# First layer: the next tile's rows turned behind the first gate half, loaded ahead of the weights, their row weights picked at the clip; the head norm behind the outputs

## The chip, the core and the metric

The kernel runs on one core of a Trainium2 chip. Times are device microseconds (us) of one execution. The engines are PE (matmul, with its weight loads shown as PEld), DVE (vector), ACT (scalar), POOL (GpSimd) and SP, which issues most of the DMAs. Every engine works through its own list of instructions in order; a semaphore wait holds back everything behind it on that engine. The clock of PE has two levels here, 2.4 GHz (shown as 1.00) and 1.2 GHz (0.50).

## What is computed

Two transformer layers over 4096 tokens (8 batches of 512) of width 256. Cut to what matters here:

```python
xn = layernorm(x)
x = x + L0_attn(xn) + L0_ffn(xn)     # first layer
xn = layernorm(x)
x = x + L1_attn(xn) + L1_ffn(xn)     # second layer

def L0_ffn(x):                       # 8 experts, 4 per token
    gate, up = split(x @ gate_up_proj[e] + bias[e])
    gate = minimum(gate, 7.0); up = clip(up, -7.0, 7.0)
    act = (up + 1.0) * gate * sigmoid(1.702 * gate)
    return sum over the chosen e of combine[n, e] * (act @ down_proj[e] + down_bias[e])
```

L0_attn is a causal softmax attention of 16 heads of 16 dimensions, whose queries and keys are normalized per head (the head norm of the title).

## The kernel before

**Steps.** The attention of the whole program is cut into 192 steps: step G is batch n = G // 8 and pair of heads p = G % 8 (the first 64 steps are the first layer's attention). The tokens of the first layer's experts lie sorted by expert in 71 tiles of 256 rows. The tiles are worked on inside the steps 21 to 49: `pipeline` writes a list `plan` of 15 pieces for each step, in six parts. The pieces of tile s are, in this order: gate half 0, up half 0, gate half 1, down half 0 of tile s-1, up half 1, down half 1 of tile s-1. As 15 pieces are two and a half tiles, the steps alternate: an **even** step (22, 24, ... 48) has the parts [down 1, gate 0], [up 0, gate 1, down 0], [up 1, down 1], [gate 0, up 0, gate 1], [down 0, up 1], [down 1, gate 0, up 0]; an **odd** one (23, 25, ... 49) [gate 1, down 0], [up 1, down 1, gate 0], [up 0, gate 1], [down 0, up 1, down 1], [gate 0, up 0], [gate 1, down 0, up 1]. Even steps have p = 6, 0, 2, 4, odd ones p = 7, 1, 3, 5.

**PE** (`pair_with_experts` in its part of `pipeline`) does in a step: `shifted` (turns the queries, source qst), `outputs_by_rows` (turns the last step's outputs, source oT), part 0, three score units (L605), `turn_qk` (turns the next step's queries, qst, and keys, kst), part 1, the other scores, part 2 and so on, then `outputs` (L681), the last part, and in the middle of that, for p = 1 to 4, `project` (L628, two matmuls for the next batch). With p = 1 it also turns the next batch's rows (`turn_rows`, source xb) behind the outputs. A gate or up half is `up()`: 12 matmuls (L539) into the bank of gate or up; a down half is 12 matmuls (L559).

**Two banks for everything that is turned.** All turns and projections write to the ring X, which in these steps has only the two PSUM banks 0 and 1, taken by turns (`take`). PE waits at each until the engine that reads the bank has let go of what was there before.

**The next tile's rows.** `turn_x(s+1)` turns the rows of the next tile (source xs, L513) into such a bank behind up half 0 of tile s. ACT copies them (`take_x`, xh), and DVE then subtracts (`rest`, xl, L1648), which frees the bank.

**DVE** does for a tile half g: `clip_gate` (L1660), `clip_up` (L1674) and `multiply` (L1683, L1686), where `multiply` runs in `finish()`, ahead of the next gate half's clip or at fixed places of the step. Behind the multiply of half 0 `finish` does `rest(s+1)`, behind that of half 1 `pick_weight(s+1)` (L1640, L1643), which waits for the gate and up weights of tile s+1 (tile gu). In a step: `heads_out` (L1931 to L1937, frees the bank of the turned outputs), for p = 0 `context_out` (L1945) and `row_stats` (L1729 on), the parts 0 and 1, ..., maxima of the scores (L1845), `shift`, the rest of the parts, and at the end for p = 0 `normalize` (L1747, four instructions on xb) and for p = 5 and 6 `norm_heads` (L1794, L1799, L1802; 4 heads, then 12).

**SP** issues the loads: rows of tile s+2 (xs) at up half 0, its gate and up weights (gu, 2 MB, once the multiply of half 1 of tile s is done) at up half 1, its down weights (dn) and the store of the outputs (ys) at down half 1.

Of the kernel before, what the change touches and what calls it, by code (L numbers as in the profile page):

```python
# [34 lines left out]
H, HD = 16, 16  # L35
# [113 lines left out]
def build(nc, dram, outs, ctx):  # L149
# [232 lines left out]
    def pipeline(kinds, its, mems, em=None, general=False):  # L382
# [39 lines left out]
        def last_tile(s):  # L422
            return s + 1 in (FIRST_TILE[1], FIRST_TILE[1] + TILES[1])

        def tiles_to(s):
            return FIRST_TILE[layer_of(s)] + TILES[layer_of(s)]
# [65 lines left out]
        with block as block:  # L492

            @block.tensor
            def _(pe):
# [25 lines left out]
                def up(s, m, side):  # L521
# [18 lines left out]
                                           x[s % 2][:, TS * k:TS * (k + 1)],  # L540
                                           start=(n == 0), stop=(n == len(terms) - 1))
                    mm.then_inc(full, 1)
                    if m == 0 and side == 1 and not last_tile(s):
                        turn_x(s + 1)

                def down(s, half):
# [351 lines left out]
            def _(sp):  # L898
# [55 lines left out]

                def experts(G, q, some=slice(None)):
                    for what, s, i in plan[G][q][some]:
                        if what == "up" and s + 2 < tiles_to(s):
                            if i == 0:
                                load_x(s + 2)
                            else:  # L960
                                load_up(s + 2)
                        if what == "down" and i == 1:
                            if s + 2 < tiles_to(s):
                                load_down(s + 2)
                            store_y(s)
# [399 lines left out]
            def _(act):  # L1365
# [38 lines left out]

                def experts(G, q, some=slice(None)):
                    for what, s, i in plan[G][q][some]:
                        if what == "up":
                            highs()
                            gate(2 * s + i)
                            late.append(2 * s + i)  # L1410
                            if i == 0 and not last_tile(s):
                                take_x(s + 1)
                        elif what == "down":
                            highs()
                            take_y(s, i)
# [214 lines left out]
            def _(dve):  # L1630
# [65 lines left out]
                def experts(G, q, some=slice(None)):  # L1696
                    for what, s, i in plan[G][q][some]:
                        if what == "gate":
                            finish()
                            if layer_of(s) == 0:  # L1700
                                clip_gate(2 * s + i)
                        if what == "up":
                            if layer_of(s) == 0:
                                clip_up(2 * s + i)
                            late.append((s, i))

                def finish():

                    while late:
                        s, i = late.pop(0)  # L1710
                        multiply(2 * s + i)
                        if not last_tile(s):
                            if i == 0:
                                rest(s + 1)
                            else:
                                pick_weight(s + 1)
# [397 lines left out]
                def pair_with_experts(G):  # L2114
# [2 lines left out]
                        heads_out(G - 1)  # L2117
                    if is_at(n - 1, "mla") and p == 0:
                        context_out(n - 1)
                    if G in begins:  # L2120
                        rest(FIRST_TILE[begins.index(G)])
                        pick_weight(FIRST_TILE[begins.index(G)])
# [20 lines left out]
                        residual(n - 1)  # L2143
                    if n + 1 < nb and p == 0:
                        normalize(n + 1)
                    if is_at(n + 1, "mla"):
                        if p == 5:
                            norm_heads(n + 1, slice(0, 4))
                        if p == 6:
                            norm_heads(n + 1, slice(4, H))  # L2150

                def pair_alone(G):
                    n, p = divmod(G, NP)
# [321 lines left out]
```

## Time and profile before

| | us |
|---|---|
| median of 3 runs | 3187.16 |
| lowest and highest | 3186.24, 3191.06 |
| profiled execution, whole | 3193.81 |
| profiled execution, span of the core | 3192.2 |
| PE busy in the span | 2821.9 (88%) |
| DVE busy | 2168.8 (68%) |
| ACT busy | 1621.9 (51%) |
| POOL busy | 1496.9 (47%) |

Times of the trace are counted from the start of the span. The first layer's expert steps, 21 to 49, lie between 430 and about 1350 us. A line of the timeline is a group of like instructions in a row: its start, the time from its start to its end, engine, line, operation, output<-input, shapes and count, and in brackets how long the engine stood idle before it and what ended that.

### The profile page before, as it was taken

Reading aid. Unit: us, or ns where it says so; the run is one execution under the profiler, and the core shown is the slowest. Engines: PE = TensorE matmul, PEld = TensorE weight load, DVE = VectorE, ACT = ScalarE, POOL = GpSimd, SP = SyncE. Lnnn points to the kernel's source line nnn. Section 1 sums busy time; section 2 is a strip of 40 time slices with the busy share of each in tenths; the row PEclk is TensorE's granted clock in tenths of the full one; section 3 lists DMA queues with packets and bytes.
Section 4 is the critical chain, followed back from the end, with each engine's and each line's share of the span. In section 5 each row is a group of like instructions: output and inputs, shape, how many; then the busy total and the mean of one; then the engine's idle time right before and its main releaser. Section 6 shows DMA issues by size and latency. Waiting matters only on the chain. (4 is left out here: it accounts for less than half of the span.)

```text
span 3192.2 us, 60490 instructions
## 1 busy us (share of the span) xinstructions
PE 2821.9 (88%) x20990; PEld 2283.0 (72%) x20990; DVE 2168.8 (68%) x6229; ACT 1621.9 (51%) x3388; POOL 1496.9 (47%) x2213
## 2 busy tenths in 40 slices
PE   3878789999999999978898889898799999999986
PEld 2555478888989898846666666666588888888864
DVE  4777678778778787756777777766645554454576
ACT  1544444544444454445655555555455555555553
POOL 3586753353343353375556666322233333333487
PEclk8877799999999999989999999999899999999998
DMA  2564567778777787522333444210365555565445
GB/s 81 179 218 165 199 246 290 276 280 320 281 283 285 280 298 297 216 40 51 94 93 106 107 107 107 91 67 21 134 221 207 212 214 211 199 234 204 134 96 123
DMA packets 192066, 580.08 MB, mean 182 GB/s; under 512 B 22856, under 2 KB 144656, under 8 KB 157456
## 3 DMA queue, kind: packets, MB, share of 16 engines
q1 hardware_dynamic: 154896, 525.03, 44.6%
q0 software_dynamic: 36864, 51.14, 7.8%
q8 instruction: 172, 2.82, 0.3%
q14 instruction: 134, 1.10, 0.1%
HBM read 450.14 MB, written 125.96 MB: 180 GB/s over the span
## 5 line engine op out<-in xcount | busy, mean ns | idle before, releaser
L1157 POOL TENSOR_TENSOR al<-t,ah 128x512 fp32r<-128x512 f32 x220 | 285.5, 1298 | 865.9 <-ACT ah L1389 865.9
L539 PE MATMUL bank<-xh,gu 128*128 128x256 f32 x3520 | 658.0, 291 | 22.7 <-DMA gu<-wu_scratch 7.0
L584 PE MATMUL bank<-masks_bf,ident_bf 128*128 128x128 bf16 x1896 | 433.3, 252 | 131.8 <-DVE st L1845 41.4
L1845 DVE TENSOR_REDUCE st<-bank 128x1 f32<-128x512 f32 (+3 forms) x1024 | 422.7, 480 | 181.8 <-PE bank L602 152.9
L539 PEld LDWEIGHTS bank<-xh,gu 128*128 128x128 f32 x3520 | 512.8, 192 | 45.1 <-issue 19.1
L1486 ACT ACTIVATE pt<-bank 128x512 f32<-128x512 f32 (+1 forms) x1152 | 512.3, 541 | 47.5 <-PE bank L605 40.2
L1494 ACT ACTIVATE oT<-bank 128x512 f32<-128x512 f32 x192 | 114.5, 597 | 615.3 <-PE bank L681 581.9
L584 PEld LDWEIGHTS bank<-masks_bf,ident_bf 128*128 128x128 bf16 x1896 | 170.5, 99 | 356.5 <-DVE st L1845 99.7
L602 PE MATMUL bank<-ksT,qsT 128*128 128x512 f32 (+3 forms) x1536 | 412.6, 369 | 5.8 <-DVE top L1843 3.2
L605 PE MATMUL bank<-qaT,ksT 128*128 128x512 f32 (+3 forms) x1536 | 402.7, 372 | 0.0
L539 PE MATMUL bank<-xl,gu 128*128 128x256 f32 x1760 | 354.6, 283 | 0.0
L602 PEld LDWEIGHTS bank<-ksT,qsT 128*128 128x128 f32 x1536 | 279.2, 203 | 27.8 <-DVE top L1843 17.1
L513 PE MATMUL bank<-ident,qst 128*128 128x128 f32 x1536 | 239.3, 284 | 57.8 <-POOL kst L1209 35.4
L1389 ACT ACTIVATE ah<-t 128x512 fp32r<-128x512 f32 x220 | 138.7, 630 | 286.9 <-DVE t L1686 249.6
L539 PEld LDWEIGHTS bank<-xl,gu 128*128 128x128 f32 x1760 | 273.7, 192 | 0.0
L605 PEld LDWEIGHTS bank<-qaT,ksT 128*128 128x128 f32 x1536 | 267.9, 201 | 6.1
L1843 DVE MAX8 top<-bank 128x8 f32<-128x512 f32 (+3 forms) x512 | 213.7, 483 | 72.7 <-PE bank L602 50.1
L681 PE MATMUL bank<-pt,V 128*17 128x512 f32 (+3 forms) x3072 | 261.0, 460 | 0.7 <-ACT pt L1486 0.7
L559 PE MATMUL bank<-dn,ah 128*128 128x256 f32 x1760 | 257.0, 288 | 0.0
L513 PEld LDWEIGHTS bank<-ident,qst 128*128 128x128 f32 x1536 | 184.9, 146 | 91.5 <-issue 41.0
L559 PEld LDWEIGHTS bank<-dn,ah 128*128 128x128 f32 x1760 | 224.7, 191 | 4.6 <-issue 3.7
L1262 POOL DMA_INDIRECT acc<-ys_scratch,slots x128 | 203.5, 1590 | 45.0 <-issue 39.2
(254 smaller groups left out, 5247.0 us busy)
## 6 DMA issues: line engine op xcount, KB each, us to landing
gu<-wu_scratch SPq DMA_DIRECT2D x110, 2056.0 KB, 8.0
dn<-wd_scratch SPq DMA_DIRECT2D x110, 1024.0 KB, 9.7
xs<-xs_scratch SPq DMA_DIRECT2D x110, 264.0 KB, 9.0
ys_scratch<-yb SPq DMA_DIRECT2D x110, 256.0 KB, 9.9
raw<-in_gu SPq DMA_DIRECT2D x16, 1024.0 KB
wu_scratch<-hi SPq DMA_DIRECT2D x16, 1024.0 KB
wu_scratch<-lo SPq DMA_DIRECT2D x16, 1024.0 KB
xs_scratch<-empty SPq DMA_DIRECT2D x32, 264.0 KB
```

Of the source, the lines that this page charges most:

```text
L513: mm = pe.transpose(bank[:, P * n:P * (n + 1)], b, ident[:, :])
L539: mm = pe.matmul(bank[:, TS * h:TS * (h + 1)], gu[:, col:col + P], x[s % 2][:, TS * k:TS * (k + 1)], start=(n == 0), stop=(n == len(terms) ...
L559: mm = pe.matmul(down_bank[:, D * half:D * (half + 1)], a[s % 2][:, j // 2, tok:tok + P], dn[:, part + D * j:part + D * (j + 1)], start=(n ...
L584: return pe.matmul(S.bank((which, G, u))[:, diag:diag + P * len(unit)], ident_bf[:, :], masks_bf[:, side, 0:len(unit), :].rearrange("p n k ...
L602: mm = pe.matmul(bank[:, first:first + width], mem["qsT"][:, P * blk:P * (blk + 1)], ks[:, 0:width], start=begin, stop=end, skip_group_che ...
L605: mm = pe.matmul(bank[:, first:first + width], ks[:, P * blk:P * (blk + 1)], mem["qaT"][:, T - width:T], start=begin, stop=end, skip_group ...
L681: mm = pe.matmul(bank[q0:q0 + HD + 1, P * kb:T], V[n % 2][:, kb, vh, :], pt[:, j, PT_AT[kb]:PT_AT[kb] + T - P * kb], start=(kb < 2), stop= ...
L1157: pool.tensor_tensor(em["al"][s % 2][:, m, :], em["t"][g % 2][:, :], em["ah"][s % 2][:, m, :].bitcast(F32), ALU.subtract).then_inc(al_read ...
L1262: pool.indirect_dma_start(acc[:, NT * b + t, :], None, ys_dram, at, compute_op=ALU.add).then_inc(gathered[i], 16)
L1486: act.activation(to, frm, ACT.Relu if kind == "spm" else ACT.Exp).then_inc(s_act, 1)
L1843: ins = dve.max(top[:, 0, r, :], bank[:, first:first + width])
L1845: ins = dve.reduce_max(st[:, 0, r:r + 1], bank[:, first:first + width], AX.X)
```

## The change

- `turn_x(s+1)` stands behind gate half 0 of tile s instead of up half 0 (first layer only), and `take_x` on ACT moves with it, ahead of that half's tanh.
- On DVE `rest(s+1)` comes right behind `clip_gate` of half 0, and `pick_weight(s+1)` right behind `clip_up` of half 1, ahead of the multiply of that half; `finish` does neither in the first layer any more.
- SP loads the rows of tile s+3 at up half 1 of tile s, ahead of the weights of tile s+2.
- `norm_heads` of the next batch moves from the end of the steps p = 5 and 6 to the steps p = 6 and 7, behind `heads_out` (and `context_out`).

```diff
@@ PE, up() @@
-                    if m == 0 and side == 1 and not last_tile(s):
+                    if m == 0 and side == layer_of(s) and not last_tile(s):
                         turn_x(s + 1)
@@ SP, experts() @@
-                        if what == "up" and s + 2 < tiles_to(s):
-                            if i == 0:
-                                load_x(s + 2)
-                            else:
+                        if what == "up" and i == 0 and (layer_of(s) or s == 0) and s + 2 < tiles_to(s):
+                            load_x(s + 2)
+                        if what == "up" and i == 1:
+                            if layer_of(s) == 0 and s + 3 < tiles_to(s):
+                                load_x(s + 3)
+                            if s + 2 < tiles_to(s):
                                 load_up(s + 2)
@@ ACT, experts() @@
+                        if what == "gate" and i == 0 and layer_of(s) == 0 and not last_tile(s):
+                            highs()
+                            take_x(s + 1)
                         if what == "up":
                             highs()
                             gate(2 * s + i)
                             late.append(2 * s + i)
-                            if i == 0 and not last_tile(s):
+                            if i == 0 and layer_of(s) and not last_tile(s):
                                 take_x(s + 1)
@@ DVE, experts() and finish() @@
                                 clip_gate(2 * s + i)
+                                if i == 0 and not last_tile(s):
+                                    rest(s + 1)
                         if what == "up":
                             if layer_of(s) == 0:
                                 clip_up(2 * s + i)
+                                if i == 1 and not last_tile(s):
+                                    pick_weight(s + 1)
                             late.append((s, i))
...
-                        if not last_tile(s):
+                        if layer_of(s) and not last_tile(s):
                             if i == 0:
                                 rest(s + 1)
@@ DVE, pair_with_experts() @@
                     if is_at(n - 1, "mla") and p == 0:
                         context_out(n - 1)
+                    if is_at(n + 1, "mla"):
+                        if p == 6:
+                            norm_heads(n + 1, slice(0, 4))
+                        if p == 7:
+                            norm_heads(n + 1, slice(4, H))
...
-                    if is_at(n + 1, "mla"):
-                        if p == 5:
-                            norm_heads(n + 1, slice(0, 4))
-                        if p == 6:
-                            norm_heads(n + 1, slice(4, H))
```

**PE, start of an even step.** From the end of gate half 0 in part 0 (into bank2) over the first scores to up half 0 (bank3). Before:

```order
L539 MATMUL bank2<-xh1_103,gu1_107 128x256 x2
L605 MATMUL bank5<-qaT_57,ksT00_53 128x512
L605 MATMUL bank6<-qaT_57,ksT00_53 128x128
L605 MATMUL bank6<-qaT_57,ksT00_53 128x384
L605 MATMUL bank7<-qaT_57,ksT00_53 128x256
L513 MATMUL bank1<-ident,qst1_50 128x128 x4
L513 MATMUL bank0<-ident,kst_51 128x128 x4
L539 MATMUL bank3<-xh1_103,gu1_107 128x256 x2
```

Now:

```order
L539 MATMUL bank2<-xh1_103,gu1_107 128x256 x2
L513 MATMUL bank1<-ident,xs0_100 128x128 x4
L605 MATMUL bank5<-qaT_57,ksT00_53 128x512
L605 MATMUL bank6<-qaT_57,ksT00_53 128x128
L605 MATMUL bank6<-qaT_57,ksT00_53 128x384
L605 MATMUL bank7<-qaT_57,ksT00_53 128x256
L513 MATMUL bank0<-ident,qst1_50 128x128 x4
L513 MATMUL bank1<-ident,kst_51 128x128 x4
L539 MATMUL bank3<-xh1_103,gu1_107 128x256 x2
```

The turn of xs moved ahead of the scores. It takes bank1, the bank that the queries took, so that the queries now take bank0, which the outputs (oT) had, and the keys (kst) take bank1, which xs has.

**PE, end of an even step with a projection.** From the last matmuls of gate half 0 over L628 to the first turns of the next step. Before:

```order
L539 MATMUL bank2<-xh1_103,gu1_107 128x256 x2
L628 MATMUL bank0<-w_mla_72,xT 128x512
L628 MATMUL bank1<-w_mla_72,xT 128x512
L539 MATMUL bank3<-xh1_103,gu1_107 128x256 x2
L539 MATMUL bank3<-xl1_105,gu1_107 128x256 x2
L539 MATMUL bank3<-xh1_103,gu1_107 128x256 x4
L539 MATMUL bank3<-xl1_105,gu1_107 128x256 x2
L539 MATMUL bank3<-xh1_103,gu1_107 128x256 x2
L513 MATMUL bank0<-ident,xs0_100 128x128 x4
L513 MATMUL bank1<-ident,qst1_50 128x128 x4
L513 MATMUL bank0<-ident,oT_59 128x128 x4
```

Now:

```order
L539 MATMUL bank2<-xh1_103,gu1_107 128x256 x2
L513 MATMUL bank0<-ident,xs0_100 128x128 x4
L628 MATMUL bank1<-w_mla_72,xT 128x512
L628 MATMUL bank0<-w_mla_72,xT 128x512
L539 MATMUL bank3<-xh1_103,gu1_107 128x256 x2
L539 MATMUL bank3<-xl1_105,gu1_107 128x256 x2
L539 MATMUL bank3<-xh1_103,gu1_107 128x256 x4
L539 MATMUL bank3<-xl1_105,gu1_107 128x256 x2
L539 MATMUL bank3<-xh1_103,gu1_107 128x256 x2
L513 MATMUL bank1<-ident,qst1_50 128x128 x4
L513 MATMUL bank0<-ident,oT_59 128x128 x4
```

The second of the two projections (L628) now takes bank0, which xs took just ahead; the outputs (oT) at the start of the next step take a bank that the projection had, where before they took that of xs.

**DVE, from the last multiply of a step with p = 5 into the step with p = 6.** Before:

```order
L1683 SCALAR_TENSOR_TENSOR gc_92<-th_93,gc_92 128x512
L1686 SCALAR_TENSOR_TENSOR t1_95<-t1_95,gc_92 128x512
L1640 TENSOR_TENSOR wtmp_99<-xs1_101,gu1_107 128x16
L1643 TENSOR_REDUCE wsel2_98<-wtmp_99 128x2
L1794 TENSOR_TENSOR qk_mla0_66<-qk_mla0_66,qkn_73 128x4x64 x2
L1799 TENSOR_TENSOR qk_mla0_66<-qk_mla0_66,qkw_74 128x4x64 x2
L1802 TENSOR_TENSOR qk_mla0_66<-qk_mla0_66 128x4x64
L1931 COPY both_65<-bank0 128x136
L1932 TENSOR_TENSOR both_65<-both_65,bank0 128x102
L1936 RECIPROCAL rec_64<-both_65 128x8
L1937 TENSOR_TENSOR ctxt1_62<-both_65,rec_64 128x4x32
L1660 TENSOR_SCALAR gc_92<-bank2,gu1_107 128x256 x2
```

Now (the lines of the file have moved by 5 to 9):

```order
L1688 SCALAR_TENSOR_TENSOR gc_92<-th_93,gc_92 128x512
L1691 SCALAR_TENSOR_TENSOR t1_95<-t1_95,gc_92 128x512
L1940 COPY both_65<-bank0 128x136
L1941 TENSOR_TENSOR both_65<-both_65,bank0 128x102
L1945 RECIPROCAL rec_64<-both_65 128x8
L1946 TENSOR_TENSOR ctxt1_62<-both_65,rec_64 128x4x32
L1803 TENSOR_TENSOR qk_mla0_66<-qk_mla0_66,qkn_73 128x4x64 x2
L1808 TENSOR_TENSOR qk_mla0_66<-qk_mla0_66,qkw_74 128x4x64 x2
L1811 TENSOR_TENSOR qk_mla0_66<-qk_mla0_66 128x4x64
L1665 TENSOR_SCALAR gc_92<-bank2,gu1_107 128x256 x2
L1653 TENSOR_TENSOR xl0_104<-bank1,xh0_102 128x512
L1679 TENSOR_SCALAR t0_94<-bank3,gu1_107 128x256 x2
```

The two rows of `pick_weight` (wtmp, wsel) now stand just ahead of these rows, ahead of the multiply (gc, t) and behind the clip of the up half; `heads_out` (both, rec, ctxt) stands ahead of the head norm (qk_mla); and xl stands behind the clip of the gate half, with the head norm, the multiply and `heads_out` all in front of it.

## Rows read from the trace of the kernel before

**Rows 1.** who PE waited for between 430 and 1345 us: total, times, longest.

```profile
PE bank L513 <- DVE xl L1648: 28.8, 14, 2.1
PE bank L513 <- DVE both L1932: 9.6, 7, 1.6
PE bank L539 <- DMA gu<-wu_scratch: 7.0, 8, 1.8
PE bank L539 <- DVE gc L1660: 6.9, 16, 1.6
PE bank L513 <- DVE xb L1747: 3.9, 3, 2.7
```

**Rows 2.** windows: length, busy us (instructions) by engine, PE clock, DMA share, GB/s.

```profile
430.00:1345.00 915.00, 856.59 (x6960) 805.00 (x6961) 709.03 (x1621) 439.59 (x863) 361.76 (x473) 0.98 0.75 282
...
755.00:759.00 4.00, 4.00 (x35) 3.92 (x33) 3.96 (x4) 0.84 (x2) 1.52 (x1) 1.00 0.93 376
...
821.00:825.00 4.00, 4.00 (x23) 4.00 (x22) 0.85 (x3) 1.70 (x3) 1.27 (x1) 0.58 0.87 329
```

**Rows 3.** timeline, PE, step 21.

```profile
439.48 0.66 PE L513 MATMUL bank<-ident,kst 128*128 128x128 f32 x4 [1.38 <-DVE xl L1648]
```

**Rows 4.** timeline, DVE, from step 30 into step 31 (p = 7).

```profile
752.49 0.68 DVE L1683 SCALAR_TENSOR_TENSOR gc<-th,gc 128x512 f32<-128x512 f32 x1
...
753.82 0.68 DVE L1648 TENSOR_TENSOR xl<-bank,xh 128x512 fp32r<-128x512 f32 x1
...
754.42 2.91 DVE L1794 TENSOR_TENSOR qk_mla<-qk_mla,qkn 128x768 f32<-128x768 f32 x2
...
760.10 0.29 DVE L1931 COPY both<-bank 128x136 f32<-128x136 f32 x1
...
761.29 0.88 DVE L1660 TENSOR_SCALAR gc<-bank,gu 128x256 f32<-128x256 f32 x2
```

**Rows 5.** timeline, PE, step 49 (p = 1), with no xs turned before it.

```profile
1338.07 1.16 PE L513 MATMUL bank<-ident,xb 128*128 128x128 f32 x8 [2.71 <-DVE xb L1747]
```

**Rows 6.** timeline, PE and DVE, start of step 30 (p = 6).

```profile
723.85 0.50 PE L539 MATMUL bank<-xh,gu 128*128 128x256 f32 x2 [0.28 <-DMA gu<-wu_scratch]
...
723.90 0.17 DVE L1640 TENSOR_TENSOR wtmp<-xs,gu 128x16 f32<-128x16 f32 x1 [0.40 <-DMA gu<-wu_scratch]
...
724.20 1.85 DVE L1794 TENSOR_TENSOR qk_mla<-qk_mla,qkn 128x256 f32<-128x256 f32 x2
...
727.22 0.29 DVE L1931 COPY both<-bank 128x136 f32<-128x136 f32 x1
...
727.86 0.66 PE L513 MATMUL bank<-ident,kst 128*128 128x128 f32 x4 [1.25 <-DVE both L1932]
```

**Rows 7.** timeline, PE and DVE, start of step 32 (p = 0).

```profile
787.86 0.50 PE L539 MATMUL bank<-xh,gu 128*128 128x256 f32 x2 [0.76 <-DMA gu<-wu_scratch]
...
789.22 0.29 DVE L1931 COPY both<-bank 128x136 f32<-128x136 f32 x1
...
793.59 0.88 DVE L1660 TENSOR_SCALAR gc<-bank,gu 128x256 f32<-128x256 f32 x2
...
794.52 0.51 PE L539 MATMUL bank<-xh,gu 128*128 128x256 f32 x2 [1.59 <-DVE gc L1660]
```

**Rows 8.** timeline, POOL, DVE and PE, start and end of step 26 (p = 2).

```profile
597.41 1.29 POOL L1157 TENSOR_TENSOR al<-t,ah 128x512 fp32r<-128x512 f32 x1 [5.11 <-ACT ah L1389]
...
597.73 1.12 DVE L1937 TENSOR_TENSOR ctxt<-both,rec 128x128 f32<-128x128 f32 x1
...
598.88 0.88 DVE L1660 TENSOR_SCALAR gc<-bank,gu 128x256 f32<-128x256 f32 x2
...
599.06 0.60 PE L513 MATMUL bank<-ident,kst 128*128 128x128 f32 x4
...
621.34 1.88 PE L628 MATMUL bank<-w_mla,xT 128*128 128x512 f32 x4
```

**Rows 9.** loads of gu, xs: count, KB, median us; then times of gu.

```profile
gu<-wu_scratch SPq DMA_DIRECT2D x110, 2056.0 KB, 8.0
...
xs<-xs_scratch SPq DMA_DIRECT2D x110, 264.0 KB, 9.0
...
DMA to landing us min/median/max: 7.5/8.0/14.2
```

## The prediction

> **What bounds the kernel now.** The change touches only the steps 21 to 49, so I read first how PE stands there. In 915 us it is busy 856.6, at a mean clock of 0.98, with DVE at 709 and the DMA queues at 0.75 [rows 2]: PE sets the pace, and a gain can only come from its idle time and its slow clock. Next, who it waits for [rows 1]: 28.8 us in 14 waits for xl, the step that frees the bank of the next tile's turned rows; 9.6 in 7 for the bank of the last outputs (both, L1932); 7.0 in 8 for the gate and up weights; 6.9 in 16 for the clip of a gate half; 3.9 for the normalized rows (xb). That is 56 us, the ceiling for waits. The xl waits are nearly one number: 28.8 less the 1.38 of step 21 [rows 3] leaves 13 waits of 2.1, one at the start of each odd step from 23 to 47. There xs was turned last in the even step before, and the outputs need its bank two turns later.
>
> Third, the clock: a window of 4 us in step 31 holds 35 matmuls at 1.00, one in step 33 only 23 at 0.58 [rows 2]. The mean of 0.98 over 915 us is some nine such stretches, each costing about 4 x 0.42 = 1.7 us; the shown one follows a start of an odd step. So a wait of 2 us at times costs nearly twice.
>
> **The durations I use.** A half of 12 matmuls takes 12 x 4.00/35 = 1.4 us [rows 2]. On DVE the multiply takes 1.33 us (752.49 to 753.82), `heads_out` 1.19 (760.10 to 761.29), a gate clip 0.88, xl 0.68, the large head norm 5.68 (754.42 to 760.10) [rows 4], the small one 3.02 (724.20 to 727.22) [rows 6], `heads_out` with `context_out` and `row_stats` 4.37 (789.22 to 793.59) [rows 7]. Weights land 7.5 to 8.0 us after issue [rows 9].
>
> **What is taken away.** All 13 waits at odd steps (27.4 us) and that of step 21 lose their cause: xl has the whole up half to finish in. What is late next differs:
> - p = 1 (steps 25, 33, 41): PE turns the next batch's rows there, and these wait for `normalize`. Step 49, which has no xs before it, shows the wait without xl: 2.71 us [rows 5]. Only what xl took out of DVE's chain is won, 0.68 less the 0.4 by which the up half now ends later: 0.3 us each, 0.9.
> - p = 3 and 5 (6 steps): the even step before projects. The second L628 now takes the bank of xs; in step 26 both start right behind the gate half, at 621.34 [rows 8]. xs takes 0.4 and the first L628 0.65, so PE wants the bank 1.05 after the gate half's end; clip and xl alone need 1.56, ACT's copy in between may add 0.5. The wait is 0.5 to 1.1; I take 1.0. Won: 1.1 each, 6.6.
> - p = 7 (4 steps): PE gets ahead, but `heads_out`, the large norm and the next clip stay one row on DVE: from the multiply's end at about 754.3 they end at 754.3 + 1.19 + 5.68 + 0.8 = 762. PE reaches the next gate half at 760 and waits 2 us, where it now waits 1.55 at the keys (one of the waits for both). Further on, `pick_weight` holds DVE until the next weights are in, 7.9 us behind a multiply that came only 0.6 earlier. I put the gain at 1.1 of 3.7: 4.4.
> - step 21: xl falls under the up half, 1.2.
>
> Sum: 13.1 us won. The waits of 0.2 for a clip, one in each odd step, only move into the waits for weights.
>
> **What is added.** At the start of all 14 even steps xs is now turned between the outputs and the next queries. With two banks taken in turn, the keys then need the bank of xs, and PE waits there for xl, with up half 0 and all behind it queued. The trace has this pattern once: in step 21 the keys wait 1.38 us for xl [rows 3]. In the even steps it is worse, since xl now stands on DVE behind `pick_weight`, multiply, `heads_out` and the gate clip.
> - p = 6 (4 steps), on the clock of step 30: the weights are in at 723.85 and `pick_weight` waits for them until 723.90 [rows 6]. Now the multiply stands behind it: 724.2 + 1.33 + 1.19 + 3.02 (norm) + 0.88 + 0.68 = 731.3. The keys ran at 727.86, the wait for both included. 3.4 us later, less the 0.4 of xs, which no longer stands behind the up half: 3.0 each, 12.0.
> - p = 0 (4 steps), on the clock of step 32: weights 787.9, + 0.3 + 1.33 + 4.37 + 0.88 + 0.68 = 795.5; keys 0.4 and up half 1.4 put gate half 1 at 797.3, where it ran at 794.52 after a wait of 1.59 [rows 7]. 2.8 here, more where that wait was shorter: 3.1 each, 12.4.
> - p = 2 and 4 (6 steps): nothing between `heads_out` and the clip, and the weights come in time. In step 26 the clip starts at 598.88; 0.8 and 0.68 put xl at 600.3 against keys at 599.06 [rows 8]: 1.3, less 0.4, 0.9 each, 5.4. Of this 0.8 is the 1.12 us that L1937 took beside POOL's subtraction, which ended just before it, against 0.3 elsewhere.
>
> The Trainium skill (SBUF — State Buffer, Who interferes with whom) calls the port pair that DVE and GpSimd share an exclusive lock, which the loser waits for whole. By that rule L1937 is held only if POOL starts first; the cost in these six steps would be 1.3 or 0.5 less 0.4, so the sum moves by 5 us at most. The trace agrees as far as it goes: L1937 ended 0.15 us behind POOL's instruction [rows 8].
>
> Sum: 29.8 us lost.
>
> **The rest at nothing.** SP's load of rows costs some 1 us of the queue (264 of 2056 KB of 8 us [rows 9]). Where weights are waited for, the multiply behind `shift` triggers them some 4 us after `pick_weight` let the rows go, so the rows are through; if not, 8 waits grow by 1: +8. ACT's copy goes ahead of a tanh by 0.6 us, and DVE has the clip of the up half to do meanwhile. The head norm ends 1 us later, and POOL, which stacks its result, needs the next keys' turn first anyway.
>
> **The clock.** Of the nine slow stretches five follow xl waits that vanish (p = 3, 5, 7). If 5 of 13 waits of 2.1 us bring one, waits of some 4 us should nearly always, so I give the eight at p = 6 and 0 one each, of which one place has it already. Two more than now, 3.4 us; between -8 (none new) and +15. The Trainium skill (TensorE: Matmul & The Clock Gate, Part 1) says that idling throttles the array and sustained work releases it. By that rule alone each of the eight waits would bring a stretch, the same +3.4; that 8 of the 13 waits of 2.1 us brought none here says that a wait alone does not decide it.
>
> **Sum:** -13.1 + 29.8 + 3.4 = +20 us. On the profiled execution that is 3193.8 + 20 = 3213.8; it lies 6.6 above the median, so for the median I say 3187.2 + 20 = 3207.
>
> **Rivals.**
> 1. *Faster: the keys don't wait.* If xl ends before PE is through xs, scores and the queries' turn, 1.4 us behind the gate half, nothing is added, and five slow stretches go: -13 - 8 = -21, 3166; with the waits for both gone too, down to 3150. It decides at DVE's lead at the start of the even steps. Against it: `pick_weight` at 723.90 and the clip at 793.59 [rows 6, 7] show DVE behind PE there, and step 21 shows the wait. 0.12.
> 2. *No change.* If the weights came 1.8 us earlier at p = 6 and 0, the multiply would not be held: 8 x 1.8 = 14 less, and without new slow stretches the sum is 0 to +5, about 3190. Against it: 7.5 us is the shortest landing [rows 9], and the multiply that triggers them does not come earlier. 0.12.
> 3. *Slower, clock and queue.* Each long wait brings two stretches, and rows ahead of weights add to the waits: +15 + 8, 3225. 0.12.
>
> **Chances.** Forecast, 3194 to 3219, 0.64. Range: 3184 to 3224, which leaves out the fast rival and half of the third. 0.2% is 6.4 us, about what a measurement can tell from none. Slower 0.76, same 0.12, faster 0.12.
>
> **What would show it.** PE's waits for xl stay near 30 us, but sit at the keys (ident,kst) in the 14 even steps, 3 to 4.5 us at p = 6 and 0, under 1.5 at p = 2 and 4, and at the second L628 about 1 us in 6 steps; at the outputs' turn none is left. Step 49 still waits 2.7 for xb. The waits for both all but vanish. The clock over 430 to 1360 us stays at 0.97 or 0.98. Wrong would be: keys that wait less than 1.5 us at p = 6 and 0, or odd steps that win more than 2 us each.

## The result: 1.3% slower

| | before | after |
|---|---|---|
| median, us | 3189.11 (4 runs) | 3231.64 (4 runs) |
| lowest and highest | 3186.24, 3191.06 | 3224.92, 3234.34 |
| span of the profiled execution | 3192.2 | 3223.4 |

The ratio is 1.0129, with a 95% interval of 1.0106 to 1.0151: 42 us slower by the medians, where 20 were forecast and 3224 was the end of the range. The sign and the place were right; the loss was forecast at half its size.

**The profile after.** First the waits of PE in the stretch of the expert steps (engine, line and what it waited for: us in total, times, longest); they answer to [rows 1]:

```profile
PE bank L513 <- DVE xl L1653: 49.8, 14, 5.5
PE bank L539 <- DVE gc L1665: 11.6, 9, 2.6
PE bank L513 <- DVE xb L1756: 10.9, 4, 2.7
PE bank L539 <- DMA gu<-wu_scratch: 7.4, 9, 1.7
PE bank L628 <- DVE xl L1653: 3.3, 6, 0.6
```

The waits for xl are 49.8 us instead of 28.8, and the longest is 5.5 instead of 2.1. The bank of the outputs (both) has gone from the list, a new line is L628 for xl, 6 times, and the waits for xb have grown.

The lines by window (length, busy us and instructions of PE, PEld, DVE, ACT and POOL, clock of PE, DMA share, GB/s). The first is from the first gate half of step 21 to the turn of xb in step 49, which in the kernel before is 432 to 1338 us. The second holds one of the new waits:

```profile
430.00:1376.00 946.00, 861.04 (x6905) 809.33 (x6906) 720.79 (x1611) 427.99 (x851) 367.60 (x465) 0.97 0.75 273
...
538.00:548.00 10.00, 7.25 (x43) 7.21 (x43) 5.67 (x17) 2.55 (x5) 3.55 (x9) 0.66 0.71 274
```

The stretch is 40 us longer (945.6 against 906.0), which is the whole loss; outside it the two executions differ by 8 us the other way. The mean clock fell from 0.98 [rows 2] to 0.97, and around the wait of step 24 it is 0.66.

Timeline of PE, DVE and POOL at the start of step 30 (p = 6), the place of [rows 6] (start, us, engine, line, operation, output<-input, in brackets the idle time before and what ended it):

```profile
732.46 0.51 PE L539 MATMUL bank<-xh,gu 128*128 128x256 f32 x2 [0.61 <-DMA gu<-wu_scratch]
...
732.51 0.17 DVE L1645 TENSOR_TENSOR wtmp<-xs,gu 128x16 f32<-128x16 f32 x1 [2.05 <-DMA gu<-wu_scratch]
...
732.81 0.68 DVE L1688 SCALAR_TENSOR_TENSOR gc<-th,gc 128x512 f32<-128x512 f32 x1
...
734.14 0.29 DVE L1940 COPY both<-bank 128x136 f32<-128x136 f32 x1
...
734.96 1.28 POOL L1159 TENSOR_TENSOR al<-t,ah 128x512 fp32r<-128x512 f32 x1 [4.62 <-ACT ah L1391]
...
735.00 1.39 DVE L1946 TENSOR_TENSOR ctxt<-both,rec 128x128 f32<-128x128 f32 x1
...
736.42 0.76 DVE L1803 TENSOR_TENSOR qk_mla<-qk_mla,qkn 128x256 f32<-128x256 f32 x2
...
738.35 0.87 DVE L1665 TENSOR_SCALAR gc<-bank,gu 128x256 f32<-128x256 f32 x2
...
739.14 0.68 DVE L1653 TENSOR_TENSOR xl<-bank,xh 128x512 fp32r<-128x512 f32 x1
...
739.88 0.82 PE L513 MATMUL bank<-ident,kst 128*128 128x128 f32 x4 [4.21 <-DVE xl L1653]
```

This is the chain that was forecast. `pick_weight` runs at 732.51, as soon as the weights are in; the multiply stands behind it, then `heads_out` (734.14), the head norm (736.42), the clip (738.35) and xl (739.14). PE has the keys' turn next and waits 4.21 us. From the weights to the keys are 7.42 us (732.46 to 739.88), where they were 4.01 (723.85 to 727.86 in [rows 6]): 3.4 later, as worked out, though two of the parts are not what was worked out (see below).

The same at p = 0 (step 32), the place of [rows 7], and the gate clip and xb at p = 7 and p = 1:

```profile
774.84 0.86 DVE L1665 TENSOR_SCALAR gc<-bank,gu 128x256 f32<-128x256 f32 x2
...
775.85 0.47 PE L539 MATMUL bank<-xh,gu 128*128 128x256 f32 x2 [2.52 <-DVE gc L1665]
...
800.37 0.18 DVE L1645 TENSOR_TENSOR wtmp<-xs,gu 128x16 f32<-128x16 f32 x1 [2.18 <-DMA gu<-wu_scratch]
...
802.82 1.27 POOL L1159 TENSOR_TENSOR al<-t,ah 128x512 fp32r<-128x512 f32 x1 [4.70 <-ACT ah L1391]
...
802.85 1.39 DVE L1946 TENSOR_TENSOR ctxt<-both,rec 128x128 f32<-128x128 f32 x1
...
804.27 1.23 DVE L1954 TENSOR_TENSOR acc<-acc,ctxt 128x1024 f32<-128x1024 f32 x1
...
805.53 1.41 DVE L1738 BATCH_NORM_STATS2 stats<-xb 128x6 f32<-128x256 f32 x4
...
807.47 0.88 DVE L1665 TENSOR_SCALAR gc<-bank,gu 128x256 f32<-128x256 f32 x2
...
809.00 1.11 PE L513 MATMUL bank<-ident,kst 128*128 128x128 f32 x4 [5.46 <-DVE xl L1653]
...
837.67 1.16 PE L513 MATMUL bank<-ident,xb 128*128 128x128 f32 x8 [2.72 <-DVE xb L1756]
```

The keys wait 5.46 us here. L1946, the last step of `heads_out`, takes 1.39 us. The same instruction in the same step of the kernel before, from its timeline:

```profile
790.07 0.29 DVE L1937 TENSOR_TENSOR ctxt<-both,rec 128x128 f32<-128x128 f32 x1
```

It took 0.29. The turn of the keys takes 1.11 us, where it takes 0.60 in [rows 8]: a stretch at half clock begins at 808.5, in the wait.

### The profile page after: what moved, and what is told of

It is laid out like the page before. It is cut to its first block and busy times, and to the rows that moved or that the text cites. A ratio compares the mean times of both kernels' runs of the same rounds, so it can differ in the third digit from the quotient of the medians.

```text
span 3223.4 us, 60498 instructions
## 1 busy us (share of the span) xinstructions
PE 2824.9 (88%) x20990; PEld 2290.3 (71%) x20990; DVE 2186.5 (68%) x6229; ACT 1616.7 (50%) x3388; POOL 1506.3 (47%) x2213
## 5 line engine op out<-in xcount | busy, mean ns | idle before, releaser
L539 PE MATMUL bank<-xh,gu 128*128 128x256 f32 x3520 | 665.6, 294 | 29.0 <-DVE gc L1665 11.6
L539 PEld LDWEIGHTS bank<-xh,gu 128*128 128x128 f32 x3520 | 520.9, 195 | 51.9 <-issue 29.9
```

Source lines behind the costliest of these rows:

```text
L539: mm = pe.matmul(bank[:, TS * h:TS * (h + 1)], gu[:, col:col + P], x[s % 2][:, TS * k:TS * (k + 1)], start=(n == 0), stop=(n == len(terms) ...
```

## The experiments

The runs of e1 to e4 shared one chip, with a median of 3172.4 us for the kernel before; e5 to e8 a second (3191.0), e9 to e12 a third (3192.1). So all are given as a ratio to the kernel before in the same call, with the 95% interval in brackets; the us behind it are that ratio of the kernel before. Where the two medians differ by another number, by 3 us or more, it is given too. On this scale the changed kernel stands at 1.0129, and on the third chip (e12) at 1.0152. Diffs are against the changed kernel unless it is said otherwise, and cut to what matters.

**Theory A** is that of the prediction: in the even steps the keys now take the bank of xs, so PE waits for DVE's chain from the multiply to xl, and these long waits bring slow clock. The rivals are that the chain is long because of something else (pick_weight, the moved norm), or that the waits would only move.

### e1: the keys ahead of xs

```diff
@@ PE, even steps from 22 on @@
 experts(G, 0)              # turn_x of this part is kept back
 scores("k", G, range(NU // 2))
 turn_qk(G + 1)
+turn_x(kept)               # behind the keys
@@ ACT @@
 take_qk(G + 1)
+take_x(kept)
```

> The changed kernel with one edit: in the 14 even steps from 22 on, the first turn of xs (and ACT's copy of it) stands behind the turn of the keys instead of ahead of the scores, so that the keys take the bank that the outputs left. Theory A (the keys wait for xl in the even steps, and these waits also bring slow clock): the 49.8 us of PE's waits for xl nearly vanish; gate half 1 then waits for the late clip, some 2.5 us at p = 0 and 1 us at p = 6, 14 us in all; slow stretches fall to some 10. 3231.6 - 50 + 14 - 12 = 3184 us, 3175 to 3192. Theory B (the waits follow from a DVE that is late, whatever it is that PE waits for): the waits only change their name, 3220 to 3232.

Measured: ratio 0.9993 (0.9982 to 1.0005), 2 us below the kernel before. This one edit takes back the whole loss, so the place of xs at 14 starts of even steps is its cause. The waits of PE in it:

```profile
PE bank L541 <- DVE gc L1682: 19.1, 21, 2.5
PE bank L513 <- ACT qsT L1487: 17.1, 13, 1.5
PE bank L513 <- DVE xb L1773: 10.9, 4, 2.7
```

No wait for xl is left there. Theory B has its share: 19.1 us are waits for the clip, up from 11.6, and 17.1 are a wait that I had not named. With xs right behind the keys, its turn needs the bank of the queries just turned and waits for ACT's copy of them.

### e2: pick_weight behind the multiply again

```diff
@@ DVE @@
 clip_up(2 * s + 1)
-pick_weight(s + 1)
@@ finish() @@
 multiply(2 * s + 1)
+pick_weight(s + 1)
@@ SP @@
-load_x(s + 3)              # at up half 1
+load_x(s + 2)              # at up half 0
```

> The changed kernel with pick_weight back behind the multiply and the loads of rows back where they were (rows of tile s+2 at up half 0). Theory A (half of the chain that the keys wait for is the multiply that pick_weight holds until the weights land): the multiply, 1.37 us, leaves that chain; the waits for xl at p = 6 fall from 4.2 to 2.9 us and those at p = 0 from 5.5 to 4.1, with a little clock 3231.6 - 8 x 1.4 - 5 = 3216 us, 3208 to 3224. Theory B (the multiply is held as long anyway, by its own inputs): 3228 to 3234. Theory C (pick_weight at the clip is the cause of the whole loss): 3190.

Measured: ratio 1.0114 (1.0091 to 1.0137), 36 us above the kernel before. On the first chip's 3189 that is 3225 us, 3218 to 3233, between A (3208 to 3224) and B (3228 or more). The time does not decide between those two, and the waits show that neither describes this kernel:

```profile
PE bank L513 <- DMA xs<-xs_scratch: 38.5, 31, 2.8
PE bank L539 <- DVE gc L1663: 11.0, 6, 2.6
PE bank L513 <- DVE xl L1651: 11.0, 11, 3.6
```

The waits for xl did fall, by more than forecast, to 11.0 us. But the rows of the next tile, loaded as late as in the kernel before and turned one half earlier, are now late at 31 turns, 38.5 us in all. So the early load of the rows, which I had put at nothing, is needed by the early turn. That the early load in turn needs pick_weight done early, as the rows lie in two buffers, is argued and not shown: e7 below has the early load with pick_weight behind the multiply, the rows then loaded behind the weights, and PE never waits for rows there.

### e3: the turn of xs where it was

```diff
@@ PE @@
-if m == 0 and side == layer_of(s) and not last_tile(s):
+if m == 0 and side == 1 and not last_tile(s):
     turn_x(s + 1)
@@ ACT, DVE: take_x and rest back behind the up half, too @@
```

> The changed kernel with the turn of xs, its copy and its subtraction back behind up half 0; the early pick_weight, the early load of rows and the moved head norm stay. Theory A (the early turn is what costs): the waits for xl are 2.1 us at 13 odd steps again and none at the keys; the waits for both go (the head norm is out of their way), but the clip of gate half 1 comes 1.3 to 2.4 us later at p = 6 and 0 and 1.5 later at p = 7, some 10 to 15 us in all: 3200 us, 3190 to 3210. Theory B (pick_weight and norm carry the loss): 3220 to 3232.

Measured: ratio 1.0044 (1.0027 to 1.0061), 14 us above the kernel before.

```profile
PE bank L513 <- DVE xl L1650: 28.9, 14, 2.1
PE bank L539 <- DVE gc L1662: 19.2, 17, 2.8
```

Theory A, and near its number: the waits for xl are back at 28.9 us, those for both are gone, and the waits for the clip are 19.2 where they were 6.9 [rows 1]. That is the price of pick_weight ahead of the multiply and of the norm ahead of the clip, the two together.

### e4: the head norm where it was

```diff
@@ DVE, start of the step @@
-if p == 6: norm_heads(n + 1, slice(0, 4))
-if p == 7: norm_heads(n + 1, slice(4, H))
@@ DVE, end of the step @@
+if p == 5: norm_heads(n + 1, slice(0, 4))
+if p == 6: norm_heads(n + 1, slice(4, H))
```

> The changed kernel with the head norm back at the end of the steps p = 5 and 6. Theory A: the small head norm still stands between the multiply and xl, so the keys at p = 6 wait 4.2 us as before this edit; at p = 7 the wait of 2.5 us for the clip becomes one of 1.5 us for both at the keys and about 1 for the clip. Within 5 us of the changed kernel, 3231.6. Theory D (the moved norm is what made p = 7 lose 7.5 us): 3222.

Measured: ratio 1.014 (1.0118 to 1.0161), against 1.0129 and 1.0152 for the changed kernel: the moved norm gave and cost nothing that can be told.

```profile
PE bank L513 <- DVE xl L1653: 36.8, 14, 5.5
PE bank L513 <- DVE both L1941: 25.6, 8, 3.8
```

The two lines together are 62.4 us, where the changed kernel has 49.8 and 11.6 for the clip. The waits changed their names more than their sum (88.1 us in all, against 83.3): at p = 6 the queries now wait 2.7 us for both and the keys 1.35 for xl, together 4.0 where the keys alone waited 4.2. At p = 7 the keys wait 3.7 us for both, more than the 1.5 and 1 that I gave for that place.

### e5: the same banks, a shorter chain

```diff
@@ DVE, even steps from 22 on @@
 heads_out(G - 1)
+rest(s + 1)
 context_out / norm_heads / row_stats
 clip_gate(2 * s)
-rest(s + 1)
```

> The changed kernel with one edit on DVE: in the even steps from 22 on, the subtraction of xl stands right behind heads_out, ahead of the head norm, context_out, row_stats and the clip. Banks and PE's order stay. Theory A (the wait at the keys is as long as the work on DVE between the multiply and xl): xl comes 2.7 us earlier at p = 6, 3.5 to 4 at p = 0, 0.9 at p = 2 and 4, so PE's waits for xl fall from 49.8 to about 20 us and slow clock falls with them; the kernel before plus 0 to 8 us, where the change gave plus 42. Theory B (the order of the banks costs by itself, or ACT's copy sets the time of xl): plus 30 to 42.

Measured: ratio 1.0022 (1.0008 to 1.0037), 7 us above the kernel before. Theory A; with PE's order and banks unchanged, 34 of 41 us have gone.

```profile
PE bank L539 <- DVE gc L1665: 22.7, 18, 2.6
PE bank L513 <- DVE xl L1653: 17.4, 13, 1.5
```

So it was the length of the chain, not the order of the banks as such. Of the 32 us won on xl 11 came back as waits for the clip (22.7 us): what stands ahead of the clip holds PE next.

### e6: the first xs of the even steps behind the up half

```diff
@@ all engines @@
+late_tiles = tiles whose gate half 0 stands in part 0
-side == layer_of(s)
+side == (layer_of(s) or s in late_tiles)
```

> The changed kernel with the first turn of xs in the even steps from 22 on, its copy and its subtraction back behind up half 0, where the kernel before has them; the second one of each even step and that of the odd steps stay behind gate half 0. Theory A: the keys take the bank of the outputs, and the 17.1 us that PE waited for the copy of the queries with the turn right behind the keys go too; the clip's waits of some 19 us stay. The kernel before minus 15 us, minus 8 to minus 20. Theory B (PE only gets to the late clip earlier and waits there): minus 0 to 5.

Measured: ratio 0.9997 (0.9984 to 1.0011), 1 us below the kernel before. Theory B.

```profile
PE bank L542 <- DVE gc L1668: 28.3, 21, 2.8
```

No wait for xl or for the queries is left at the starts of the steps, and nothing is won: PE gets to the clip sooner and waits 28.3 us there. I had left the clip's waits at 19 though PE had 17 us less to wait ahead of them. DVE was the pace there, so its chain was the next thing to shorten.

### e7: the clip ahead of the batch work

```diff
@@ against e6: DVE @@
 heads_out(G - 1)
+experts(G, 0)
 context_out / norm_heads / row_stats
-experts(G, 0)
@@ pick_weight behind the multiply, load_x(s + 3) behind load_up(s + 2) @@
```

> The kernel of the last expectation with two more edits in the first layer: pick_weight back behind the multiply, the rows of tile s+3 loaded behind the weights of tile s+2; and on DVE the pieces of part 0 ahead of context_out, the head norm and row_stats. Theory A (what is left is a clip that DVE reaches late, and weights that are loaded late because the multiply was held for the last ones): waits for gc fall from some 19 to 9 us, for gu from 9 to 3, and nearly no slow clock: another 12 us, the kernel before minus 27 us, minus 18 to minus 35. Theory B (the head norm, now behind the clip, holds the clip of the up half and gives all back): within 5 us of the last kernel.

Measured: ratio 0.9905 (0.9884 to 0.9926), 30 us below the kernel before (34 by the medians). Theory A in its size.

```profile
PE bank L516 <- DVE xb L1757: 10.9, 4, 2.7
PE bank L542 <- DMA gu<-wu_scratch: 7.9, 8, 1.9
PE bank L542 <- DVE gc L1668: 6.3, 17, 0.7
PE bank L631 <- DVE xl L1656: 3.3, 6, 0.6
```

The waits for the clip fell from 28.3 to 6.3 us. Those for the weights did not fall (7.9 instead of 3), so that part of the reasoning was wrong. Theory B's wait, the clip of the up half behind the large norm, is small: 2.9 us in 4 waits (not in the rows above). The two edits were not tried apart.

### e8: the rows of the batch turned behind part 0

```diff
@@ against e7: PE, and take_rows on ACT the same way @@
-turn_rows(n + 1)
 experts(G, 0)
+turn_rows(n + 1)
```

> The kernel of the last expectation with the turn of the next batch's rows (xb) behind part 0 in the first layer's steps with p = 1. Expected: PE's waits of 2.7 us for xb at 4 steps nearly go, 8 to 10 us less than the last kernel: the kernel before minus 36 us. The rival: normalize ends later now that row_stats is later, and PE waits for xb behind part 0 as long: within 3 us of the last kernel.

Measured: ratio 0.9874 (0.9849 to 0.9899), 40 us below the kernel before (44 by the medians), the best kernel of the study. By windows, the whole stretch of the expert steps:

```profile
429.00:1290.00 861.00, 836.20 (x6920) 786.52 (x6920) 714.16 (x1609) 428.97 (x852) 379.12 (x466) 1.00 0.79 299
```

861 us instead of 906, at a clock of 1.00: the only time at half clock left is 2.8 us at the start of step 21. The waits for xb are 4.7 us where e7 has 10.9.

### e9: one wait made longer

```diff
@@ against the kernel before: DVE, rest(s), 13 places @@
+xl = bank - xh             # twice more
+xl = bank - xh
 xl = bank - xh
```

> The kernel before with one wait made longer: where xs is turned last in an even step (13 places), the subtraction of xl is done three times in a row, so that the outputs at the start of the next odd step wait some 1.5 us longer, 3.6 instead of 2.1. That alone is 13 x 1.5 = 19 us. Theory A (a longer wait brings slow clock more often, which is the part of the loss that the prediction sized too small): some six more stretches of slow clock, 1.7 us each, plus 29 us, 25 to 36. Theory B (the slow stretches have nothing to do with the length of a wait): plus 19 us, 16 to 22.

Measured: ratio 1.0095 (1.0058 to 1.0131), 30 us above the kernel before (25 by the medians). The interval, 19 to 42 us, holds the forecast of A and reaches into that of B, so the time alone does not decide; the trace does. Timeline of PE in it, one of the 13 places:

```profile
772.63 1.09 PE L516 MATMUL bank<-ident,oT 128*128 128x128 f32 x4 [3.56 <-DVE xl L1655]
```

Each of the 13 waits is 3.56 us, and at 11 of the 13 places the turn behind it takes 1.08 or 1.09 us, at half clock, where it takes 0.63 at full clock. The trace records when the granted clock changes: a stretch at half clock begins in or within 1.1 us behind each of the 13 waits, 65 us in all with the one in step 21. The first trace of the kernel before has 34, and e11, on the chip of this run, 13. That is theory A: a longer wait brings slow clock more surely.

The 13 waits grew by 19 us in all and PE's waits together by 14, for those for both shrank by 5. Of the 31 us more at half clock PE spent 9 idle, where the clock costs nothing, so they cost 11 us. Together that is 25, and the stretch of the expert steps is 24 us longer than in the first trace of the kernel before (31 longer than in e11).

### e10: e8 without the early turn

```diff
@@ against e8: PE, ACT, DVE @@
 turn_x, take_x, rest: everywhere behind the up half, as in the kernel before
```

> The kernel of e8 with the turn of xs, its copy and its subtraction everywhere where the kernel before has them: only the order on DVE (pieces of part 0 ahead of context_out, head norm and row_stats), the later turn of the rows xb, and the earlier load of xs are left. Theory A (the early turn at the odd places is worth its 13 waits of 2.1 us and the slow clock behind them, once nothing waits for it): 25 to 35 us slower than e8's minus 44, so the kernel before minus 10 to minus 20. Theory B (the early turn was never worth anything, DVE's order is all): the kernel before minus 35 to minus 45.

Measured: ratio 0.9964 (0.9949 to 0.998). Theory A: without the early turn e8 keeps 11 of its 40 us (14 of 44 by the medians). The waits for xl are back:

```profile
PE bank L513 <- DVE xl L1654: 28.8, 14, 2.1
```

So the early turn is worth some 30 us (e8 ran on the second chip, e10 on the third), at the places where e6 had left it, once the keys don't wait for it and DVE reaches the clip in time.

### e11 and e12: both kernels once more, on one chip

> The kernel before once more, unchanged, for its trace on the same chip as the other runs. 0 us; steps 21 to 49 take 912 us as in its first trace if what lies around them is all that differs between chips, less if the clock in them differs too.

> The changed kernel once more, on the same chip as the kernel before in this call. Plus 42 us, 35 to 50; in steps 21 to 49 the waits for xl are again 50 us, and slow clock some 60 us, against some 30 in the kernel before.

Measured: 1.0006 (0.9987 to 1.0026) and 1.0152 (1.0125 to 1.018), 49 us above the kernel before (44 by the medians). In the profiled executions the stretch took 899 us in e11 and 947 in e12, with 13 and 65 us at half clock: the 30 expected for the kernel before were wrong. Waits for xl in e11 and e12:

```profile
PE bank L513 <- DVE xl L1648: 28.8, 14, 2.1
```

```profile
PE bank L513 <- DVE xl L1653: 49.7, 14, 5.5
```

The waits for xl repeat to 0.1 us, but e11 is 7 us shorter there than the first trace of the same kernel. It has 13 us at half clock instead of 34: a slow stretch follows 3 of its 13 waits of 2.1 us, and 8 of 13 in the first trace. What these waits cost in idle time is fixed; what they cost in clock changes from one execution to another. Whether the chip has a part in it stays open, for the chip of the first trace is not on record; but on the one chip of e11 the eight runs of this kernel spread from 3178 to 3199 us, and the profiled one was the fastest.

## Why the prediction was wrong

The mechanism held and three terms of the sum were too small: the clock (+3.4 where the traces show +11.7), the keys at p = 2 and 4 (+5.4, measured +11.1) and the keys at p = 0 (+12.4, measured +17.8).

The length of the stretch follows one sum in all traces: some 835 us, plus PE's waits as its timeline shows them (without those for issue), plus half of the time at half clock in which PE does not wait. All in us; "idle" is the part of the time at half clock that lies in PE's waits, and the rest is the length less the other terms:

| | length | waits | at half clock | idle | rest |
|---|---|---|---|---|---|
| before | 906.0 | 56.2 | 33.9 | 0.5 | 833 |
| e11, before again | 898.7 | 56.9 | 13.3 | 0.1 | 835 |
| after | 945.6 | 83.3 | 64.2 | 7.4 | 834 |
| e12, after again | 946.9 | 86.0 | 64.9 | 8.8 | 833 |
| e1, keys first | 906.0 | 59.5 | 17.1 | 0.4 | 838 |
| e2, pick_weight back | 941.2 | 77.5 | 52.5 | 2.4 | 839 |
| e3, turn back | 918.6 | 60.6 | 46.2 | 1.3 | 836 |
| e4, norm back | 954.3 | 88.1 | 78.5 | 13.4 | 834 |
| e5, xl early | 917.0 | 62.7 | 33.7 | 0.0 | 837 |
| e6, xs late | 902.6 | 51.5 | 30.7 | 0.1 | 836 |
| e7, clip first | 869.7 | 31.3 | 13.4 | 0.8 | 832 |
| e8, rows later | 860.7 | 24.5 | 2.8 | 0.0 | 835 |
| e9, longer wait | 929.7 | 70.1 | 64.9 | 9.7 | 832 |
| e10, no early turn | 890.0 | 40.7 | 33.8 | 0.0 | 832 |

The rest stays between 832 and 839, while the length goes from 861 to 954. So the 39.6 us between the first two traces are 27.1 of waits and 11.7 of clock. The prediction had 16.7 and 3.4. By its own terms (us; measured is the wait after less that of before):

| term | predicted | measured |
|---|---|---|
| step 21 | -1.2 | -1.3 |
| p = 1, 3 steps | -0.9 | +0.7 |
| p = 3 and 5, 6 steps | -6.6 | -9.4 |
| p = 7, 4 steps | -4.4 | -3.0 |
| p = 6, 4 steps | +12.0 | +11.9 |
| p = 0, 4 steps | +12.4 | +17.8 |
| p = 2 and 4, 6 steps | +5.4 | +11.1 |
| other small waits | 0 | -0.6 |
| clock | +3.4 | +11.7 |
| sum | +20 | +39 |

- **What is bounded, and where the waits go: right.** All waits for xl at the odd steps went and came back at the keys of the 14 even steps; the second L628 waits 0.55 us in 6 steps, and both is gone. e1 shows that the place of xs does it, e5 that the chain on DVE sets the size.
- **p = 6: right to 0.1 us, in part by luck.** The order of the chain was right, and so was the unknown, that the multiply stands behind the weights. But two durations were wrong by 1.1 us each, and they cancel. `heads_out` took 2.28 us (734.14 to 736.42), not 1.19, as at p = 0 below. The small head norm took 1.93 (736.42 to 738.35), not 3.02: [rows 6] has its first two instructions at 1.85 us, and they stood beside POOL's subtraction there, where they take 0.76 now that nothing of POOL's runs. The line of POOL in the kernel before:

```profile
724.24 1.52 POOL L1157 TENSOR_TENSOR al<-t,ah 128x512 fp32r<-128x512 f32 x1 [3.41 <-ACT ah L1389]
```

- **p = 0: the term "787.9, + 0.3 + 1.33 + 4.37 + 0.88 + 0.68 = 795.5" was short by 1.1 us a step.** 4.37 for `heads_out`, `context_out` and `row_stats` was read where L1937 took 0.29 [rows 7]. Now it starts 0.03 us behind POOL's subtraction and takes 1.39. I knew this pair from [rows 8] and weighed it only where it stood already, not where the change would bring it: the multiply, whose result POOL waits for through ACT, now stands right ahead of `heads_out`, without `pick_weight` between them. The other 0.25 us a step is not taken apart.
- **p = 2 and 4: "the weights come in time" failed.** From the timeline of step 26, after:

```profile
603.83 0.60 PE L513 MATMUL bank<-ident,oT 128*128 128x128 f32 x4
...
604.91 0.18 DVE L1645 TENSOR_TENSOR wtmp<-xs,gu 128x16 f32<-128x16 f32 x1 [0.44 <-DMA gu<-wu_scratch]
...
605.21 0.68 DVE L1688 SCALAR_TENSOR_TENSOR gc<-th,gc 128x512 f32<-128x512 f32 x1
...
607.39 1.40 DVE L1946 TENSOR_TENSOR ctxt<-both,rec 128x128 f32<-128x128 f32 x1
...
610.36 0.66 PE L513 MATMUL bank<-ident,kst 128*128 128x128 f32 x4 [1.58 <-DVE xl L1653]
```

  `pick_weight` waits for the weights here too, and the multiply starts 1.38 us behind the turn of the outputs, where it started 0.56 behind it before (594.70 and 595.26). With 0.3 more in L1946 and the rest of the chain as forecast, the six waits are 1.54 to 2.35 us instead of 0.9. `pick_weight` waits in all six of these steps, 0.36 to 1.32 us, and the longest of PE's waits stand where it waits longest.
- **p = 3, 5, 7 and 1: the right rivals for what is late next, with errors of 0.3 to 0.5 us a step**, the wait at L628 0.55 where I took 1.0, that for the clip at p = 7 2.52 where I took 2 (there `heads_out` took 2.31 us instead of 1.19, and the large norm 5.12 instead of 5.68).
- **The clock: the largest single miss, 8 us.** The eight waits at p = 6 and 0 brought a stretch each, as assumed. But three of these stretches were twice as long, and six more followed waits of 2.2 to 2.7 us: the clip at p = 7, xb at p = 1 (one of these, too, twice as long), the keys at p = 2. That made 30 us more at half clock instead of 7; PE was idle in 7 of them, and the other 23 cost 11.7. I had taken off what left with the waits of 2.1 us and put nothing for waits as long that the same sum said would stay or come (2 us for the clip, 2.7 for xb). The chance was misread as well: five stretches did follow the waits that were to vanish (p = 3, 5, 7), but three more followed those at p = 1, so it was 8 of the 13 waits of 2.1 us, not 5, and "8 of the 13 brought none" should have been 5. e9 bears out that longer waits bring slow clock more surely: a stretch followed all 13 waits of 3.56 us, and 11 of the 26 waits of 2.1 us in the two traces of the kernel before, not the same ones each time. The Trainium skill (TensorE: Matmul & The Clock Gate, Part 1) says that idling throttles the array; the traces agree with it, 65 us at half clock in e9 with its long waits and 3 in e8.
- **The rival "slower, clock and queue"** (3225; its terms add up to 3227) was the nearest in time. Its clock, +15, was close to the +11.7; its queue was not, for the waits for the weights stayed at 7.4 us; and it left the terms at p = 2, 4 and 0 as they were.

## What to carry to other kernels

With two banks taken in turn, a turn that is moved ahead changes who waits for whom two turns later: write down the new pairs of bank and reader, and for each the whole chain of the reader's engine in front of it. Put what the next waiter needs ahead of what only the batch needs (e7 against e6, some 30 us), and only then move the turn, where nothing waits for it at once (e8 against e10, some 30 us); made first and everywhere, the move lost 42. When durations of rows are added up, look what else ran beside each row: at p = 6 two such rows were off by 1.1 us, and only chance made them cancel. And price every wait with the clock that follows it, those that stay as well as the new ones.

## What the runs showed of the hardware

**A small DVE instruction with two inputs in SBUF, started beside POOL's 128x512 subtraction, ends with it.** L1946 (L1937 before) multiplies two tiles of SBUF into 128x128 elements. In the expert steps of the kernel before 23 of 29 took 0.29 us, and six, started 0.32 us behind POOL's start, took 1.12. In the changed kernel 24 of 29 started 0.03 or 0.04 us behind POOL's start and took 1.38 to 1.41, each ending some 0.15 us behind POOL's end (802.85 + 1.39 against 802.82 + 1.27 above). The other five, with no POOL work beside them, took 0.29. In e10, where other work stands between the multiply and `heads_out` again, 21 of 29 took 0.29; two that started 0.83 and 1.01 us behind POOL took 0.62 and 0.42, and ended 0.15 us behind it as well. The Trainium skill (SBUF — State Buffer, Who interferes with whom) says that a DVE instruction with two SBUF inputs contends with a GpSimd instruction that reads SBUF, over a shared port pair that is an exclusive lock. These numbers agree. A later place of the kernel before does not follow from it:

```profile
1364.59 5.42 POOL L1242 TENSOR_TENSOR qkn<-qkn,minus_half 128x32 f32<-128x32 f32 x1 [4.78 <-DVE qkn L1780]
...
1365.28 0.29 DVE L1937 TENSOR_TENSOR ctxt<-both,rec 128x128 f32<-128x128 f32 x1
```

L1242 is a power of 32 numbers per partition, read from SBUF too. L1937 began 0.69 us into its 5.42 us and took no longer than alone. So what POOL does counts, and not only that it is busy; why, no run here shows.

The meeting in the changed kernel is a matter of phase: from the start of `heads_out` its three short instructions take 0.86 us to L1946 (734.14 to 735.00 above), and ACT's copy of the multiply's result ends just then, so POOL starts at 734.96.

**The clock can cost nearly as much as the waits that bring it, and not the same each time.** In e9, 14 us of wait came with 31 us more at half clock than in the first trace of the kernel before, and these cost 11 us. And the same kernel, with the same 13 waits, took 899 and 906 us for the stretch in two executions, with 13 and 34 us at half clock.
